# A decoder layer on one core: the exponential one slot ahead, statistics joined and marks set on GpSimd

## The reference

```python
x = x + self_attention(layernorm(x), Wq, bq, Wk, bk, Wv, bv)     # 16 heads, 4 key groups, causal
x = x + cross_attention(layernorm(x), ctx_512, ctx_512, Wc, bc)  # 16 heads, keys = values = context
x = x + ffn(layernorm(x))
# ffn: softmax over 64 experts; best 3 of 8 expert groups by their maxima; best 6 experts in them;
# each expert takes at most 96 tokens in token order; silu(x Wg) * (x Wu) Wd, weighted; plus a shared expert
```

## Time and profile before

| | |
|---|---|
| median of three runs | 711.96 us (710.5 to 714.83) |
| profiled execution | 710.81 us, its span 709.0 us |
| busy share of the span | PE 91%, PEld 64%, DVE 66%, ACT 47%, POOL 49% |
| busy in 120:140 (self tiles) of 20 us | PE 19.27, DVE 13.85, ACT 14.54, POOL 4.53 |
| busy in 280:300 (cross tiles) of 20 us | PE 18.41, DVE 17.77, ACT 13.43, POOL 7.68 |
| second phase, first instruction of its chain | 412.25 us |

### The profile page before, as it was taken

One profiled execution on the slowest core, in us unless ns is written; L12 is line 12 of the kernel. 1 busy time (PEld: TensorE's weight loads), 2 busy tenths in 40 slices (PEclk: granted clock), 3 DMA queues, 4 the chain that ended last, 5 costly groups with the idle time before them and its releaser, 6 DMA issues. The chain is left out here.

```text
span 709.0 us, 16775 instructions
## 1 busy us (share of the span) xinstructions
PE 642.3 (91%) x6161; PEld 452.3 (64%) x6161; DVE 467.3 (66%) x1277; ACT 332.4 (47%) x634; POOL 347.3 (49%) x380
## 2 busy tenths in 40 slices
PE   3699999999879988988998989899999999999991
PEld 1366666666658766767775455576786778677760
DVE  1466676767779799898895579925555455455463
ACT  2577776776658777677663343222222212222000
POOL 5502322212452345354421257477777777787473
PEclk9899999999999999999999999999999999999996
DMA  8223223355443322232211168239999999944597
GB/s 259 33 62 92 63 58 82 87 105 112 92 102 67 79 71 63 47 86 54 62 59 37 45 187 248 63 107 235 256 249 275 248 243 262 235 75 66 129 359 263
DMA packets 144145, 94.27 MB, mean 133 GB/s; under 512 B 61552, under 2 KB 141680, under 8 KB 144064
## 3 DMA queue, kind: packets, MB, share of 16 engines
q1 hardware_dynamic: 129008, 74.58, 40.2%
q0 software_dynamic: 10400, 14.33, 11.0%
q10 hardware_dynamic: 4656, 4.29, 1.8%
HBM read 60.26 MB, written 24.50 MB: 120 GB/s over the span
## 5 line engine op out<-in xcount | busy, mean ns | idle before, releaser
L1466 POOL DMA_INDIRECT sum_d<-tk,targets x64 | 91.9, 1436 | 28.7 <-issue 12.3
L800 DVE TENSOR_REDUCE mx<-Sc 128x16 f32<-128x1024 f32 x64 | 78.2, 1222 | 29.9 <-PE Sc L447 29.7
L1286 PE MATMUL Sc<-xT,wgu_sb 128*128 128x96 f32 (+1 forms) x768 | 92.8, 271 | 0.0
L675 ACT COPY ET<-ring 128x512 f32<-128x512 f32 x128 | 68.8, 589 | 41.4 <-PE ring L459 38.9
L1286 PEld LDWEIGHTS Sc<-xT,wgu_sb 128*128 128x128 f32 (+1 forms) x768 | 87.2, 187 | 0.4 <-issue 0.4
L475 PEld LDWEIGHTS O<-vbd,ET 128*64 128x64 f32 x2048 | 66.6, 138 | 29.4 <-issue 16.1
L804 DVE TENSOR_TENSOR E<-Sc,mx 128x1024 f32<-128x1024 f32 x64 | 78.4, 1225 | 6.5
L459 PE MATMUL ring<-ident,E 128*128 128x128 f32 x512 | 69.9, 280 | 12.3 <-ACT E L714 12.3
L1459 POOL DMA_INDIRECT rows<-rows_d,tokens x64 | 64.0, 1001 | 29.1 <-issue 13.7
L475 PE MATMUL O<-vbd,ET 128*64 128x34 f32 x2048 | 73.6, 225 | 3.5 <-ACT ET L675 3.0
L447 PE MATMUL Sc<-kbd,qT 64*64 64x256 f32 x1024 | 72.5, 386 | 3.7 <-DMA kbd<-kT 3.7
(11 more groups left out here) (209 smaller groups left out, 1201.6 us busy)
## 6 DMA issues: line engine op xcount, KB each, us to landing
wgu_sb<-in_wgu_dram SPq DMA_DIRECT2D x128, 176.0 KB, 3.7
sum_d<-zeros SPq DMA_DIRECT2D x16, 524.0 KB, 5.5
kbd<-kT SPq DMA_DIRECT2D x248, 32.0 KB, 2.2
wda_sb<-in_wd_dram SPq DMA_DIRECT2D x32, 160.0 KB
wgu_sb<-sum_d SPq DMA_DIRECT2D x10, 512.0 KB, 9.8
X<-in_x_dram SPq DMA_DIRECT2D x8, 512.0 KB, 6.6
rows_d<-xhT SPq DMA_DIRECT2D x8, 512.0 KB, 2.9
out_dram<-X ACTq DMA_DIRECT2D x8, 512.0 KB, 6.7
```

Source lines behind the costliest of these rows:

```text
L675: nc.scalar.copy(ET[:, m % 2, 4 * v:4 * v + 4].rearrange("p j q -> p (j q)"), bank(name)[:]).then_inc(s_act, 1)
L800: nc.vector.reduce_max(mx[:, m % 2, :], sc, AX.X).then_inc(s_mx, 1)
L1286: last = nc.tensor.matmul(GP[e % 2][0:m, CAP * u:CAP * (u + 1)], wgu_cols[j][:, c, m0:m0 + m], xT[:, e % 2, c, :], start=c == 0, stop=c == 1)
L1466: pool.indirect_dma_start(w["sums"][e % 2], bass.IndirectOffsetOnAxis(ap=targets[:, e:e + 1], axis=0), outs[:, e % OB, :], None, compute_o ...
```

## The change

Four things change in the first phase.

First, scores, shift and exponential move one slot ahead of the transposes: slot `m` now has `scores(m+2)`, `shift(m+2)` and `exp(m+2)` beside `probs_t(m)` and `pv(m-1)`. E has three buffers. All that feeds the scores moves with them: the loops take `f = m + 1` in the place of `m` for the norms, transposes, queries, keys, values, statistics, `deviation`, `bias` and `values`, while the routing keeps `m`. The loop begins one slot earlier.

Second, `bn_aggr` is left out on VectorE. `bn_stats` gives mean and squared deviation of the even and of the odd elements; the new `scale` on GpSimd joins the two halves: nine operations a group where there were four.

Third, the marks of the kept groups and of the chosen experts are set on GpSimd, in `keep` and `weigh`, no longer on VectorE.

Fourth, semaphores and buffers follow: `ast`, `rst` and `gs2` are double.

```diff
 def ring_uses():
...
+        f = m + 1
+        if f % 4 == 1:
+            if is_self((f + 7) // 4):
+                uses.append((("XT0", (f + 7) // 4), "act"))
...
         if m % 4 == 1:
-            if is_self((m + 7) // 4):
-                uses.append((("XT0", (m + 7) // 4), "act"))
...
             if routed((m - 9) // 4):
                 uses.append((("LT", (m - 9) // 4), "dve"))
...
# TensorE
-                        last = nc.tensor.transpose(out[:, 128 * j:128 * (j + 1)], E_[:, m % 2, at:at + 128], ident[:])
+                        last = nc.tensor.transpose(out[:, 128 * j:128 * (j + 1)], E_[:, m % 3, at:at + 128], ident[:])
...
-                pe.wait_ge(s_te, 5 * (g - NG + 1))
+                pe.wait_ge(s_chosen, g - NG + 1)
...
-                if 0 <= m + 1 < 2 * NT:
-                    scores(m + 1)
+                if 0 <= m + 2 < 2 * NT:
+                    scores(m + 2)
...
# ScalarE
+                f = m + 1
+                if f % 4 == 0 and is_self((f + 8) // 4):
+                    normalize((f + 8) // 4, 0)
+                    normalize((f + 8) // 4, 1)
...
+                if f % 4 == 3 and is_cross((f + 5) // 4):
+                    normalize((f + 5) // 4, 0)
+                    normalize((f + 5) // 4, 1)
...
+                elif f % 4 == 3:
+                    if 0 <= (f + 5) // 4 < 2 * NG:
+                        keys((f + 5) // 4)
+                if 0 <= m + 2 < 2 * NT:
+                    exp(m + 2)
...
# VectorE
-                nc.vector.bn_stats(st[:, t, :], X[:, GT * (g % NG) + t, :]).then_inc(s_st, 1)
-
-            def meanvar(g, t):
                 if t == 0 and g >= 2:
                     dve.wait_ge(s_rs, g - 1)
-                dve.wait_ge(s_st, 4 * g + t + 1)
-                nc.vector.bn_aggr(mv[:, g % 2, t, :], st[:, t, :]).then_inc(s_mv, 1)
+                nc.vector.bn_stats(st[:, g % 2, t, :], X[:, GT * (g % NG) + t, :]).then_inc(s_st, 1)
...
-                if m >= 2:
-                    dve.wait_ge(s_fill, ring.filled(("TP1", m - 2)))
+                if m >= 3:
+                    dve.wait_ge(s_fill, ring.filled(("TP1", m - 3)))
...
-                dve.wait_ge(s_gm, 5 * i + 4)
-                nc.vector.tensor_scalar(gm[:], gs2[:], 0.0, None, ALU.is_lt).then_inc(s_gm, 1)
...
+                if i >= 1:
+                    dve.wait_ge(s_chosen, i)
...
-                nc.vector.tensor_scalar(wa[:, g % 2, :, key_rows(g)], tmp2[:], 0.0, None, ALU.is_lt).then_inc(s_te, 1)
...
# GpSimd
+            def scale(stats, deviation, shift, s_var, s_pow, s_ready, n):
+
+                halves = stats.rearrange("p t (h v) -> p t h v", h=2)
+                nc.gpsimd.tensor_tensor(gap[:], halves[:, :, 0, 1], halves[:, :, 1, 1], ALU.subtract).then_inc(s_var, 1)
+                nc.gpsimd.tensor_tensor(both[:], halves[:, :, 0, 1:3], halves[:, :, 1, 1:3], ALU.add).then_inc(s_var, 1)
+                pool.wait_ge(s_var, 6 * n + 1)
+                nc.gpsimd.tensor_tensor(gap[:], gap[:], gap[:], ALU.mult).then_inc(s_var, 1)
+                pool.wait_ge(s_var, 6 * n + 2)
+                nc.gpsimd.tensor_scalar(deviation, both[:, :, 1], 4.0 / E, None, ALU.mult).then_inc(s_var, 1)
+                pool.wait_ge(s_var, 6 * n + 4)
+                nc.gpsimd.tensor_tensor(deviation, deviation, gap[:], ALU.add).then_inc(s_var, 1)
+                pool.wait_ge(s_var, 6 * n + 5)
+                nc.gpsimd.tensor_scalar(deviation, deviation, 0.25, EPS, ALU.mult, ALU.add).then_inc(s_var, 1)
+                pool.wait_ge(s_var, 6 * n + 6)
+                nc.gpsimd.tensor_tensor(deviation, deviation, half_pow[:, 0:GT], ALU.pow).then_inc(s_pow, 1)
+                pool.wait_ge(s_pow, 2 * n + 1)
+                nc.gpsimd.tensor_tensor(shift, both[:, :, 0], deviation, ALU.mult).then_inc(s_pow, 1)
+                pool.wait_ge(s_pow, 2 * n + 2)
+                nc.gpsimd.tensor_scalar(shift, shift, -0.5, None, ALU.mult).then_inc(s_ready, 1)
...
-                pool.wait_ge(s_gm, 5 * (i + 1))
+                pool.wait_ge(s_gm, 4 * (i + 1))
+                nc.gpsimd.tensor_scalar(gm[:], gs2[:, i % 2, :], 0.0, None, ALU.is_lt).then_inc(s_mark, 1)
+                pool.wait_ge(s_mark, i + 1)
...
+                pool.wait_ge(s_te, 4 * (i + 1))
+                if i >= 2:
+                    pool.wait_ge(s_fill, ring.filled(("WP", g - 2)))
+                    pool.wait_ge(s_wst[g % 2], 16 * (i // 2))
+                nc.gpsimd.tensor_scalar(wa[:, g % 2, :, key_rows(g)], tmp2[:], 0.0, None, ALU.is_lt).then_inc(s_chosen, 1)
...
-                if m % 4 == 2 and is_cross((m + 6) // 4):
-                    deviation((m + 6) // 4)
-                if m % 4 == 1 and is_cross((m + 3) // 4):
-                    bias((m + 3) // 4)
+                f = m + 1
...
+                if f % 4 == 2 and is_cross((f + 6) // 4):
+                    deviation((f + 6) // 4)
+                if f % 4 == 1 and is_cross((f + 3) // 4):
+                    bias((f + 3) // 4)
                 if m % 4 == 1 and routed((m - 5) // 4):
                     route_deviation((m - 5) // 4)
```

More of the change, by code:

```diff
@@ L576, in _ @@
                         weights_t((m - 13) // 4)
[L577 to L581, removed]
                 elif m % 4 == 3:
-                    if 0 <= (m + 5) // 4 < 2 * NG:
-                        keys((m + 5) // 4)
                     if routed((m - 7) // 4):
                         xn_t((m - 7) // 4)
[L587 to L591, removed]
+                elif m % 4 == 0:
                     if routed((m - 8) // 4):
@@ new lines, in _ @@
+                if f % 4 == 3 and is_cross((f + 5) // 4):
+                    normalize((f + 5) // 4, 0)
+                    normalize((f + 5) // 4, 1)
+                if f % 4 == 0 and is_cross((f + 4) // 4):
+                    normalize((f + 4) // 4, 2)
+                    normalize((f + 4) // 4, 3)
+                if f % 4 == 1:
+                    if is_self((f + 7) // 4):
+                        xt((f + 7) // 4, 0)
+                elif f % 4 == 2:
+                    if is_self((f + 6) // 4):
+                        xt((f + 6) // 4, 1)
+                elif f % 4 == 3:
+                    if 0 <= (f + 5) // 4 < 2 * NG:
+                        keys((f + 5) // 4)
@@ new lines, in _ @@
+                if 0 <= m + 2 < 2 * NT:
+                    exp(m + 2)
+                if f % 4 == 1:
+                    if is_self((f + 3) // 4):
+                        queries((f + 3) // 4, 1)
+                    if is_cross((f + 3) // 4):
+                        xt((f + 3) // 4, 1)
+                elif f % 4 == 2:
+                    if is_self((f + 2) // 4):
+                        values((f + 2) // 4)
+                elif f % 4 == 0:
+                    if is_self((f + 4) // 4):
+                        queries((f + 4) // 4, 0)
+                    if is_cross((f + 4) // 4):
+                        xt((f + 4) // 4, 0)
@@ L768, in _ @@
                         xn_t((m - 7) // 4)
-                else:
-                    if is_self((m + 4) // 4):
-                        queries((m + 4) // 4, 0)
-                    if is_cross((m + 4) // 4):
-                        xt((m + 4) // 4, 0)
+                elif m % 4 == 0:
                     if routed((m - 8) // 4):
@@ L907, in _ @@
                     output(m - 1)
-                if 0 <= m + 1 < 2 * NT:
-                    shift(m + 1)
-                gp, gx, t = (m + 12) // 4, (m + 9) // 4, m % 4
+                if 0 <= m + 2 < 2 * NT:
+                    shift(m + 2)
+                f = m + 1
+                gp, gx, t = (f + 12) // 4, (f + 9) // 4, f % 4
                 if is_self(gp):
```

174 lines of the change are left out of this document (66 added, 108 removed).

## The result

| | before | changed |
|---|---|---|
| median of the runs | 712.33 us (4 runs, 710.5 to 714.83) | 720.66 us (4 runs, 720.08 to 721.0) |
| profiled execution, span | 710.81, 709.0 us | 720.95, 719.2 us |
| mean granted clock | 0.978 | 0.964 |

The ratio is 1.0114, with an interval of 1.0081 to 1.0146: slower by 1.1%, which is more than this kernel's noise. The forecast was 717 us in a range of 702 to 727.

A forecast was written before the change was run, and what follows sets the result against it. TensorE was taken as the bound, with VectorE nearly as full in cross tiles. Terms -6.1 + 0.9 + 1.9 + 9.0 - 2.3 = +3.4 us, plus 1.7 for one clock fall, gave 717 us, range 702 to 727.

The forecast's parts named there:

- rival 2: Gap before the product with Wc: the clock falls in every loop, 1.7 us a group, 724 to 727 us; chance 0.30.
- term D: Slots 37 to 56, where two GpSimd sets meet: 25.5 us for each four slots against 23.7, +9.0 us in all.
- The falls of the clock: TensorE gaps of some 3 us in the five cross groups: one fall in five, +1.7 us.
- A: Self tiles: the exponential one slot ahead removes the waits of the probabilities' transposes, -6.1 us.
- B: At the start: one lengthened GpSimd set ahead of the first scores, less one aggregation, +0.9 us.
- E: Slots 57 to 63: exponential wait and lower clock go, -3.9; work done ahead already paid there, +1.6: -2.3 us.
- rival 3: TensorE's wait moves to ring banks or copies instead of going: +6.1 us, 723 us; chance 0.05.
- term C: Around tile 36: TensorE waits longer for key transfers, queued behind `values` and a GpSimd set; +1.9 us.
- The marks: Two comparisons a group go from VectorE to GpSimd: cost 0, hidden by cover; without cover at the end 0.8 us.
- Rival 1: Slots 37 to 56: the meeting of sets is covered, groups take 22.3 us, about 699 us in all; chance 0.18.

## Why the prediction was right, and where its sum was not

The sign, the place and the mechanism of the loop were right; the number of falls of the clock was not. The time came out 3.7 us above the forecast and 3.3 below the 724 us at which rival 2 begins, and above the 719 us up to which the prediction would have said no change. With four falls instead of one its own sum gives 3.4 + 4 x 1.7 = 10.2 us, the measured difference of the spans; that it meets to the tenth is luck, since the terms were off both ways. By its terms, from the two profiled executions:

- **The loop (term D): right.** 25.5 us were worked out for each group, and 25.32 is what every loop without a fall takes. Piece by piece for slots 41 to 44: 247.23, the start of the product with V, to GpSimd's start at 252.42, 5.2 (5.2 forecast); two sets 6.16 (6.2); from there to the product with Wc at 263.81, 5.2 (5.1); the last slot 6.4 (6.4). A set of 3.1 us stood in the sum, and 3.1 was measured. The first routing norm waited 3.14, 2.43 and three times 1.3 us for GpSimd, where 1 to 2 were foretold. The Trainium skill, "GPSIMD Engine Reference", section 4.1, calls GpSimd about twice as slow for two inputs; by that a set would have taken an estimated 4.3 us. The trace disagrees at this size: the added steps take 0.20 us each, where VectorE's aggregation takes 0.18; it is another operation, and the nearest one at hand.
- **The falls of the clock: this step failed.** The forecast took one in five; four came. From the product with Wc to the next product with V, 2.6 us were forecast, and it was 4.51 where the clock was at 0.50 and 2.34 where it was not. The price was right (1.7 forecast, 1.9 measured each), the count was not. The argument for the low count was that work lies within the gap, which splits it in two; slot 55 shows that a gap in two pieces, 2.11 and 0.79 us, is followed by the lower level as well. I had three long waits of the trace, two of them followed by a fall, and gave the exception too much weight. The Trainium skill, "TensorE: Matmul & The Clock Gate", section "HAM oscillation", has the loop that waits once a turn and begins each turn at the lower level; the trace agrees in four loops of five, and filling the gap removed all the falls.
- **The ends (terms A, B, E): right as a sum, wrong in their shares.** Up to slot 5 the changed kernel falls 3.2 us behind (63.28 against 60.06) where the forecast had it ahead; then it gains 4.9 up to slot 32, and 5.2 in slots 57 to 63. So A and B brought -1.7 where -5.2 was forecast, and E -5.2 where -2.3 was: together -6.9 us, -7.5 forecast, and that the two errors nearly cancel is partly luck. The slot of work done ahead would explain the signs of both, being paid at the start and coming back at the end, while I had booked 1.6 us of it, and only at the end; this is argued, no run separates it. The wait for the exponential is gone in both places of the earlier trace rows, but in the first slots, as rival 3 feared, a wait of the same size came in its place, 1.7 us for the query copy.
- **The keys around tile 36 (term C):** 1.5 us lost between slots 32 and 37, 1.9 forecast. Part of it is not the term's wait but the clock: the long wait for the transfers grew from 2.69 to 3.23 us, and the lower level behind it lasted longer (0.50 from 204 to 210, in the kernel before from 210 to 212 and 0.67 in the next 2 us).
- **The marks:** 0 forecast, nothing measurable found.

The forecast, +3.4 and +1.7 us, stands against +10.2 in the span. Of the 5.1 us between them the falls account for +5.9 (7.56 - 1.7), the loop for -0.85 (8.15 - 9.0), and the rest nearly cancels. Rival 1, the covered meeting, gave 699 us for loops of 22.3; with the sets a slot apart the loops average 22.85 and the time is 697. In the changed kernel its condition did not hold: the meeting is not covered.

## What to carry to other kernels

When a stage is moved by a slot, list for each in-order engine what the moved pieces now share a slot with: here a gain of some 15 us was there, and the meeting of two short sets on an engine that is idle half the time turned it into a loss of 8. If a new gap of this size arises on TensorE in every turn of a loop, price the fall of the clock in most turns, not in one: in the runs with the two sets in one slot and no filling, a wait of 1.45 to 3.64 us for the key copies, with a second one of 0.33 to 0.79 behind it, was followed by the lower level 12 times out of 14. Length costs only where something waits: a longer set cost nothing with the sets apart, while with both in one slot shorter sets were worth 15 us and swapping two calls 12.

## What was not expected of the hardware

The same gap is not always followed by the same clock: in slots 47, 51 and 55 TensorE waited 2.1 us for the key copies and 0.79 for `oT`, and the lower level followed in the first and the third, not in the second; what tells them apart stays open. The kernel with the marks on VectorE repeats the pattern, with the same waits, in the same slots. And the wait of 1.71 us of the earlier trace rows, which the lower level followed in the kernel before, stands with the same 1.71 us in the kernel with the joined sets alone, and the clock stays at 1.00 there. In the kernel with the routing's set first the last three loops have gaps of 0.93 and 0.79 us, and none was followed by it.

GpSimd takes 0.85 us for a comparison of 256 columns that VectorE does in 0.29, but 0.20 us for a step of 4 columns, about what VectorE's aggregation took (0.18): the small steps were nearly as short as that, the wide comparison three times as long.
